# Turning attention probabilities by VectorE blocks and a DRAM round trip instead of on TensorE

## The reference

```python
xn = _layernorm(x)                                   # x: 2 x 1024 x 512
q = rmsnorm(xn @ Wq.T, q_norm_w)                     # 32 heads of 128
k = rmsnorm(xn @ Wk.T, k_norm_w)                     # 8 heads of 128
v = xn @ Wv.T
scores = einsum('bkgqd,bksd->bkgqs', qg, k) / sqrt(128)
bias = where(rel > 0, -1e30, slope * rel)            # causal, ALiBi
attn = softmax(scores + bias)
s = einsum('bkgqs,bksd->bkgqd', attn, v) ... @ Wo.T
g = silu(ffn(xn))                                    # inner width 1376
return x + s * g
```

## Time and profile before

| | |
|---|---|
| median of 3 runs | 2454.05 us (2453.86 to 2455.95) |
| profiled execution, its own time | 2455.46 us |
| its span, first to last instruction | 2453.7 us |
| mean granted TensorE clock | 0.998 |
| busy: TensorE | 2422.6 us (99%) |
| busy: VectorE | 1693.7 us (69%) |
| busy: ScalarE | 1236.1 us (50%) |
| busy: GpSimd | 756.9 us (31%) |
| DMA | 92.19 MB, 38 GB/s in the mean |
| one middle unit (between two loads of its weights) | 127.7 us |

### The profile page before, as it was taken

The page is one execution under the profiler, slowest core; times in us unless marked ns, Lnnn a source line. Parts: engine busy times, 40 slices in busy tenths (PEclk is TensorE's granted clock), DMA queues, the critical chain, the costliest instruction groups (busy, mean ns, idle before and its releaser), DMA issues.

```text
span 2453.7 us, 37432 instructions
## 1 busy us (share of the span) xinstructions
PE 2422.6 (99%) x13232; PEld 2070.7 (84%) x13232; DVE 1693.7 (69%) x3788; ACT 1236.1 (50%) x2548; POOL 756.9 (31%) x2053
## 2 busy tenths in 40 slices
PE   7999999999999999999999999999999999999998
PEld 6888888888888888878888888888888888888887
DVE  7777777777778787823377787777777777777132
ACT  4555554555545555543355555555555545545333
POOL 2323231413233323244522232323232314131443
PEclk9999999999999999999999999999999999999999
DMA  3010000000000000023320101010000000010232
GB/s 130 1 40 4 27 18 27 18 27 18 27 18 27 18 27 18 27 91 125 112 78 1 44 1 44 1 44 1 27 18 26 18 27 18 1 44 14 90 103 103
DMA packets 23289, 92.19 MB, mean 38 GB/s; under 512 B 6592, under 2 KB 6720, under 8 KB 19136
## 3 DMA queue, kind: packets, MB, share of 16 engines
q1 hardware_dynamic: 23104, 89.80, 10.5%
HBM read 85.60 MB, written 4.19 MB: 37 GB/s over the span
## 4 chain that ended last, share of the span: by engine, by line
PE 96%; DVE 2%; ACT 1%; issue 1%; POOL 0%; DMA 0%; DVEq 0%; ACTq 0%; POOLq 0%
PE out_ps L401 17%; PE score_ps L377 16%; PE out_ps L414 14%; PE qkv_ps L351 14%; PE ring_ps L388 10%; PE qkv_ps L352 7%; PE score_ps L504 5%; PE qkv_ps L504 4%; PE ring_ps L520 4%; PE ring_ps L359 2%; PE out_ps L520 1%; PE ring_ps L364 1%; PE score_ps L351 0%; DVE y L997 0%; DVE xT_lo L868 0%
## 5 line engine op out<-in xcount | busy, mean ns | idle before, releaser
L597 ACT ACTIVATE pT_hi<-ring_ps 128x512 fp32r<-128x512 f32 x576 | 344.0, 599 | 509.8 <-PE ring_ps L388 497.2
L818 DVE TENSOR_TENSOR pT_lo<-ring_ps,pT_hi 128x512 fp32r<-128x512 f32 x576 | 396.8, 690 | 90.6 <-ACT pT_hi L597 86.0
L589 ACT ACTIVATE probs<-probs,low_min 128x896 f32<-128x896 f32 (+7 forms) x512 | 395.2, 774 | 50.4 <-DVE low_min L810 50.1
L1016 POOL TENSOR_SCALAR rs_x<-sq_sum 128x5 f32<-128x5 f32 x122 | 24.8, 203 | 1128.1 <-DVE sq_sum L749 1128.1
L388 PE MATMUL ring_ps<-ident,probs 128*128 128x128 f32 x2304 | 345.6, 273 | 0.0
L388 PEld LDWEIGHTS ring_ps<-ident,probs 128*128 128x128 f32 x2304 | 281.7, 140 | 42.1
L810 DVE CUSTOM_DVE_ANT_0 probs<-score_ps,rel_sb,slope 128x512 f32<-128x512 f32 (+5 forms) x504 | 301.7, 599 | 5.7 <-PE score_ps L377 4.3
L377 PE MATMUL score_ps<-kv_hi,qT_hi 128*128 128x320 f32 (+4 forms) x760 | 275.6, 363 | 3.0 <-DVE xT_lo L868 2.0
L401 PE MATMUL out_ps<-pT_hi,kv_hi 128*128 128x512 f32 x576 | 265.8, 461 | 2.9 <-DVE pT_lo L818 2.6
L377 PE MATMUL score_ps<-kv_hi,qT_lo 128*128 128x320 f32 (+4 forms) x760 | 261.0, 343 | 0.0
L377 PE MATMUL score_ps<-kv_lo,qT_hi 128*128 128x320 f32 (+4 forms) x760 | 260.3, 342 | 0.0
(11 more groups left out here) (178 smaller groups left out, 5293.5 us busy)
## 6 DMA issues: line engine op xcount, KB each, us to landing
qkv_raw<-w_ffn_dram SPq DMA_DIRECT2D x44, 768.0 KB, 4.2
qkv_raw<-w_qkv_dram SPq DMA_DIRECT2D x15, 1536.0 KB, 6.9
o_raw<-w_o_dram SPq DMA_DIRECT2D x16, 1024.0 KB, 4.8
o_raw<-x_dram SPq DMA_DIRECT2D x4, 1024.0 KB, 6.7
out_dram<-y SPq DMA_DIRECT2D x16, 256.0 KB, 3.7
probs<-x_dram SPq DMA_DIRECT2D x3, 1024.0 KB, 7.9
qkv_raw<-w_qkv_dram SPq DMA_DIRECT2D x4, 384.0 KB, 6.6
probs<-x_dram SPq DMA_DIRECT2D x2, 512.0 KB, 4.8
```

What stands on the lines that cost most here:

```text
L589: act.activation(row, row, ACT.Exp, scale=-1.0, bias=low_min[:, i % 2, h, HEAD_CHUNKS[i] - 1:HEAD_CHUNKS[i]], accum_out=row_sum[:, i % 2, ...
L597: act.activation(pT_hi[:, n % SLOTS, :], ring_ps[:, ring_bank(r), :], ACT.Copy).then_inc(ring_high, 1)
L818: dve.tensor_tensor(out=pT_lo[:, n % SLOTS, :], in0=ring_ps[:, ring_bank(r), :], in1=pT_hi[:, n % SLOTS, :].bitcast(F32), op=ALU.subtract) ...
```

## The change

TensorE no longer turns the probabilities, nor q and k of any tile but the first two of each row. Instead:

- VectorE transposes the 32x32 blocks of each head in place (`turn_blocks`, four instructions a tile, written `dve.transpose`), in a layout in which the four heads' blocks lie side by side. SyncE writes the tile to DRAM in rows of 2 KB (`turned_out`), waits until it has landed, and reads it back in four DMAs of 32 partitions each per group of up to 4 chunks, in pieces of 512 bytes, which puts the blocks in place (`pT`, two groups of 4 chunks). q and k go the same way (`qk_out_at`, pieces of 640 bytes).
- The division moves behind `weigh`: the reciprocals go through DRAM (`rec_out_at`, written in 4-byte pieces) and come back broadcast to 128 partitions, and `scale_att` multiplies the attention by them. `divide` (4 instructions a tile) is gone.
- `high_probs` and `low_probs` read `pT` in SBUF instead of PSUM. All low halves of the probabilities are on VectorE. The low half of the attention goes to GpSimd.
- `sum_squares` is gone: ScalarE squares each of 5 heads with a sum of its own (5 instructions for one).
- The probabilities have one buffer instead of two, so the first `bias` of a tile waits for the landing of the tile before it in DRAM (`probs_out`).
- The PSUM banks of the ring go to a third score bank and a second projection target; `project` waits for two tiles back instead of one.
- TensorE's step is written out as `project`, `out_project`, all `scores`, all `weigh`. VectorE's step is: `scale_att`, `low_qk`, `scale_qk` with its transpose, `add_y`, then the biases with the first three low halves between them, the turns, the reciprocals, and the low halves from the fourth on. In step 0 the first three low halves stand ahead of `add_y`.

```diff
+            def turn_probs(U, i):
+                t = tile(U, i)
+                slot = t % 2
+                alone(probs_turned, t * G)
...
+                sp.dma_start(turned_out[slot, 0:i + 1].rearrange("j p m -> p j m"), by_chunk[:, 0:i + 1, :]
+                             ).then_inc(probs_out, 16)
+                alone(rec_done, t)
...
+                alone(probs_out, t * 16)
+                for part in range(GROUPS_IN[i]):
...
+                    for k in range(BLOCKS):
+                        at = group % 2 * GROUP
+                        sp.dma_start(pT[k * SQUARE:(k + 1) * SQUARE, at:at + hi - lo, :]
+                                     .rearrange("r j (a m) -> r (j a) m", a=BLOCKS), there[k]).then_inc(probs_back[group % 2], 16)
...
+            def high_probs(U, i, j):
...
+                act.wait_ge(probs_back[group % 2], (group // 2 + 1) * BLOCKS * 16)
...
+            def bias(U, i, k):
...
+                if k == 0 and tile(U, i) > 1:
+                    dve.wait_ge(probs_out, (tile(U, i) - 1) * 16)
...
+            def turn_blocks(U, i, h):
+                dve.wait_ge(exped, (tile(U, i) - 1) * G + h + 1)
+                row = by_head[:, h, 0:(i + 1) * BLOCKS, :]
+                dve.transpose(row, row).then_inc(probs_turned, 1)
...
+                    for k in range(sooner, chunks):
+                        bias(U, i, k)
+                        h, part = divmod(k, HEAD_CHUNKS[i])
+                        if k - sooner < len(sooner_lows):
+                            low_probs(V, p, sooner_lows[k - sooner])
+                        if part == HEAD_CHUNKS[i] - 1 and h >= 2:
+                            turn_blocks(U, i, h - 2)
...
+                        turn_blocks(U, i, G - 2)
+                        turn_blocks(U, i, G - 1)
+                        reciprocals(U, i)
+                    for j in lows:
+                        low_probs(V, p, j)
```

More of the change, by code:

```diff
@@ L422, in step @@
+                chunks = G * HEAD_CHUNKS[i] if i < TILES else 0
+                sooner = 2 if last and i == TILES - 2 else 0
+                for k in range(sooner):
+                    scores(U, i, k, first)
+                if not (first and i < 2):
+                    out_project(U, i)
+                for k in range(sooner, chunks):
+                    scores(U, i, k, first)
                 if first and i == 0:
-                    pe.wait_ge(v_staged, tile(U, 0))
+                    turn_qk(U, 1)
@@ L472, in _ @@
+                        for t in range(HT, HT + 2):
+                            turn_x(0, t)
+                elif i <= TILES:
+                    V, p = U - (i == 0), (i - 1) % TILES
+                    for j in range(p + 1):
+                        weigh(V, p, j, None if first and i == 1 else U * TILES + i - 1)
             pe.wait_ge(ident_loaded, 16)
```

719 lines of the change are left out of this document (364 added, 355 removed).

## The result

| | kernel before | changed kernel |
|---|---|---|
| time, median of 4 runs (lowest to highest) | 2455.0 us (2453.9 to 2456.6) | 4031.3 us (4029.4 to 4034.1) |
| ratio to before, 95% interval | | 1.642 (1.639 to 1.645) |
| span of the profiled execution, mean granted clock | 2453.7 us | 4028.7 us, 0.80 |

The direction was forecast, the size was not: 2926 us was the forecast and 3280 the end of its range. 1105 us are missing from it.

What follows compares the result with a forecast made beforehand. TensorE was taken to bound the kernel; under the new order, units of 153 us (2448 for sixteen), 410 remaining span, four times 5 us at row ends and 48 us of clock gave 2926 us, range 2590 to 3280.

Steps and rivals of the forecast that it cites:

- D(n): Probabilities' round trip through DRAM, last turn to first low half: 6.2 to 13.8 us for 1 to 8 chunks.
- What bounds the kernel before, and what is removed: TensorE bounds the kernel; without the turning it alone would come down by 320 us, to 2134 us.
- VectorE's turns: Transposes on VectorE run at the bias's rate, 0.133 us per chunk plus 0.07 per instruction; 22 us a unit.
- T(8): VectorE's time for one turn instruction of 8 chunks, by T(n) = 0.133n + 0.07; four make 4.5 us a tile.
- Rival (b): Transfers or turns are dearer: half-rate reads 3120, two-cycle turns 3200, upper piece bound 3660; priced at 3240 us, chance 0.24.
- (c): Faster: turns run like the division, reads and ScalarE's extra work stay hidden; 118 us a unit, 2300 us, chance 0.05.
- Why the sums do not meet: The order keeps TensorE and VectorE from overlapping: 127 us a unit with free transfers, the whole gain gone.
- Rival (a): The reads land in time, only the order and ScalarE remain: 137 us a unit, 2600 us, chance 0.13.
- The round trip: Probabilities' write lands after 1.3 + 0.7n us, 512-byte reads cost 0.9 a chunk; reads land 2 to 3 us late.
- TensorE's clock: Idle of 2 to 4 us in nearly every step lowers TensorE's clock: 3 us a unit, 48 us.
- What would show it: Profile after: TensorE near 80%, unit about 150 us, 2 MB write landing after 7 us, clock 0.85 to 0.95.

Runs made afterwards that it cites:

- order_only: Changed kernel without the DRAM trips of the probabilities and of q and k, and with four packets of reciprocals written instead of 512: 2777.6 us.
- no_trip_rec_one: Changed kernel without the DRAM trip of the probabilities, and with four packets of reciprocals written instead of 512: 2810.8 us.
- rec_one: Changed kernel with the write of the reciprocals cut from 512 packets of 4 bytes to four from the third tile on: 3197.6 us.
- order_bare: order_only plus matmuls of zero where TensorE waits, and only 8 columns of w_o and of each w_qkv part copied from the second unit on: 2621.8 us.
- order_warm: order_only with matmuls of zero added where TensorE waits for low halves in steps 1 and 4 to 7: 2720.3 us.
- rows_warm: Changed kernel with reciprocals written as 128 packets of 16 bytes, same result, plus the matmuls of zero of order_warm: 3290.8 us.

## Why the prediction was wrong

| term | prediction | measured |
|---|---|---|
| order, engines in turn, with the clock's cost | 2442 + 48 | 2777.6 (order_only) |
| trips of the probabilities and of q and k | 416 + 20 | 33 + 387 (no_trip_rec_one and rec_one, each against the run before it) |
| the reciprocals' 512 packets | 0 | 834 |
| sum | 2926 | 4031.3 |

The prediction's sum itself goes by steps with the trips in them, and these can be set beside the traces. D(n), from the last turn of a tile of n chunks to its first low half, and the steps from last turn to last turn are distances on VectorE, medians of the middle units (us):

| D(n), n = | 3 | 4 | 5 | 6 | 7 | 8 |
|---|---|---|---|---|---|---|
| forecast | 9.4 | 11.0 | 11.7 | 12.4 | 13.1 | 13.8 |
| rec_one | 10.8 | 13.9 | 13.4 | 14.1 | 14.9 | 15.7 |
| changed kernel | 19.4 | 20.6 | 21.5 | 22.4 | 22.0 | 21.1 |

| step into a tile of | 8 | 7 | 6 | 5 | 4 | 3 | 2 | 1 | unit |
|---|---|---|---|---|---|---|---|---|---|
| forecast | 24.4 | 22.7 | 21.0 | 19.3 | 15.7 | 12.5 | 17.1 | 20.3 | 153 |
| rec_one | 26.4 | 24.6 | 23.0 | 22.4 | 16.8 | 15.5 | 20.0 | 23.4 | 172 |
| changed kernel | 33.5 | 32.7 | 31.2 | 29.0 | 25.6 | 22.3 | 21.8 | 28.3 | 224 |

What the 4-byte packets add to D(n), 5.4 to 8.6 us, is found again within 0.5 us in the step that follows (D(7) + 7.1, step into 8 + 7.1). So the chain that the prediction drew through D(n) is the one that holds, and D(n) was too short.

- **What bounds the kernel before, and what is removed**: right in kind. TensorE, 99% of the span before, is at 62% of it, and its room went to nobody.
- **VectorE's turns**: right. The row of 1024 values has 1221 ns, with the 0.08 us that a duration is longer than the distance; T(8) was 1.13. Rival (b)'s two cycles a value and (c)'s rate of the division are both out.

```profile
L857 DVE STREAM_TRANSPOSE probs<-probs 128x1024 f32<-128x1024 f32 x64 | 75.7, 1221 | 0.0
```

- **Why the sums do not meet**: the mechanism is right, the term was too small by 288 us. Its sum for free transfers walked VectorE and TensorE and took ScalarE and GpSimd as always in time. In the kernel before the copies of w_o and w_qkv lay under TensorE's work; here the step waits for them, which costs 73 us (w_o) and, by order_bare, some 26 more (w_qkv). The remaining 10 us a unit lie in all steps, 0.6 to 1.9 us in each by the medians, and no run tells what they are. Rival (a)'s 137 us a unit, "only the order and ScalarE remain", is order_bare's number, but its mechanism was that reads are hidden, and they are not.
- **The round trip**: 420 us against 436 as a difference of two kernels, which is in part luck: the forecast's unit was about 20 us too short without the trips (127 against 147) and with them (153 against 172), and the two errors cancel. Without the 4-byte packets D(n) was still 1.4 to 2.9 us too short, in the write (6.8 us to the first read of 7 chunks, forecast 6.2) and in the read (7.0 us to the high half, forecast 6.1). The piece of 512 bytes was taken too seriously, the 32 partitions were left to a rival, and the trip of q and k, which has no term in the prediction at all, is 33 us.
- **The step that failed**: D(n) = 1.3 + 0.7n + 2.5 + 0.9 min(n,4) + 0.8. It counts the write of the tile and the reads, and puts at nothing, without a reason, what the change issues between them: the write of the reciprocals. In the changed kernel D(n) is 7.3 to 10.0 us longer than that for 3 to 8 chunks, and with four packets in place of the 512 it is 1.4 to 2.9 us longer. The write is worth 834 of the 1105 us. The other 271 are steps that were too short, 16 x (172 - 153) = 304 us, less the 48 us that the forecast put on top for the clock; this count leaves 15 us open. The only row for small packets, "A packet of 20 bytes cost 8 ns", was a read, spread over 128 partitions, and was used for the pieces of the reads alone. What the write costs depends on what stands around it: 252 us without the trip of the probabilities (3062.8 - 2810.8), 834 with it (4031.3 - 3197.6), because the reads queue behind it.
- **TensorE's clock**: the size, 48 us, is near what order_warm gives back without transfers (57), and the granted clock lower than said (0.80 against 0.85 to 0.95). Whether it is on the path of the whole kernel is not shown: the same filling gave 4 us there, but hardly raised the clock (rows_warm).
- **What would show it**: the idle times and the landing of the 2 MB write (7.5 us, forecast 7) came as said; TensorE's share (62% against 80%) and the unit (223.5 against 150) did not, and the first read group of six chunks landed 14 us after the write did, not 6. None of the rivals named had this price: (b) put its highest sum, 3660, on the pieces of the reads.

The direction held for the reason that the prediction gave, that the gain is gone before any transfer is paid: the order alone is even 13% slower than the kernel before (order_only), where the forecast had it level, and the trips come on top. No version here turns it: order_bare, without the trips of the probabilities and of q and k, with nearly no weight copies and a granted clock of 0.985, is still at 2621.8 us.
